# Inverse norms from Ln and Exp on ScalarE, their product with the rotated rows on GpSimd, and other PSUM banks for two results

## What is computed

```
def attn_layer(x, Wqkv, qs, ksc, Wo):
    q, k, v = split into heads of (x @ Wqkv)
    q = l2norm(q) * qs                      # t / max(norm(t), 1e-12), over the 64 of a head
    k = l2norm(k) * ksc
    q = q * cos * scale + rotate_half(q) * sin * scale
    k = k * cos * inv + rotate_half(k) * sin * inv
    out = local_attention(q, k, v)          # softmax over 64 keys, scores times 8
    return out @ Wo
for i in range(6):
    x = attn_layer(shift_tokens(x), Wqkv[i], q_scale[i], k_scale[i], Wo[i]) + x
    x = ffn_layer(shift_tokens(x), ...) + x # layer norm, 128 -> 2 x 341, gelu gate, 341 -> 128
```

## Time and profile before

| | us |
|---|---|
| median of 3 runs | 4887.78 |
| lowest and highest | 4876.82, 4889.48 |
| the profiled execution, its own time | 4899.51 |
| its span, first to last instruction | 4897.4 |
| mean granted TensorE clock over the span | 0.928 of full speed |

### The profile page before, as it was taken

One profiled execution on the slowest core, in us unless ns is written; L12 is line 12 of the kernel. 1 busy time (PEld: TensorE's weight loads), 2 busy tenths in 40 slices (PEclk: granted clock), 3 DMA queues, 4 the chain that ended last, 5 costly groups with the idle time before them and its releaser, 6 DMA issues. The chain is left out here.

```text
span 4897.4 us, 167150 instructions
## 1 busy us (share of the span) xinstructions
PE 4225.8 (86%) x70698; PEld 3385.6 (69%) x70890; DVE 3638.9 (74%) x5894; ACT 2546.2 (52%) x3896; POOL 2850.0 (58%) x2141
## 2 busy tenths in 40 slices
PE   6996899999998999999999999999998658668667
PEld 6885677777777777777777777777775338658447
DVE  4444888888888888888888888888885564564554
ACT  2232456655555555665556555565554326546435
POOL 2223777777777777777777777777773027517025
PEclk9776999999999999999999999999999868868878
DMA  0001222222222322222222222222221021221022
GB/s 24 0 0 38 74 63 62 67 77 70 63 62 61 85 69 62 62 79 72 63 63 66 78 62 68 64 66 66 66 66 36 9 58 43 73 59 44 23 61 74
DMA packets 214198, 281.51 MB, mean 57 GB/s; under 512 B 58878, under 2 KB 103716, under 8 KB 212740
## 3 DMA queue, kind: packets, MB, share of 16 engines
q1 hardware_dynamic: 203972, 251.85, 19.9%
q0 software_dynamic: 9536, 19.55, 1.5%
HBM read 54.88 MB, written 18.28 MB: 15 GB/s over the span
## 5 line engine op out<-in xcount | busy, mean ns | idle before, releaser
L1524 POOL TENSOR_TENSOR local_rot<-local_rot,local_sines 128x512 f32<-128x512 f32 x768 | 955.2, 1277 | 889.4 <-DVE local_sines L1603 889.4
L1532 POOL TENSOR_TENSOR local_inv_norm<-local_norm2c,minus_half 128x16 f32<-128x16 f32 x384 | 1126.6, 2934 | 31.9
L1411 ACT COPY local_v_tile<-local_bank 128x1024 f32<-128x1024 f32 x192 | 195.0, 1016 | 755.1 <-PE local_bank L1186 755.1
L1184 PE MATMUL local_bank<-local_wqkv_hi,local_ys_hi 128*128 128x512 f32 x1152 | 493.2, 428 | 24.8 <-POOL local_ys_lo L1515 10.4
L1260 PE MATMUL local_bank<-ident,local_normed 128*128 128x128 f32 x3072 | 405.9, 275 | 105.7 <-ACT local_probs_t L1421 90.1
L1603 DVE TENSOR_TENSOR local_rot<-local_bank,local_table 128x1024 f32<-128x1024 f32 x384 | 467.1, 1216 | 11.3 <-issue 7.0
L1593 DVE TENSOR_TENSOR local_normed<-local_rot,local_inv_norm 128x1024 f32<-128x1024 f32 x384 | 454.7, 1218 | 19.4 <-issue 11.5
L1603 DVE TENSOR_TENSOR local_sines<-local_bank,local_table 128x1024 f32<-128x1024 f32 x384 | 466.5, 1215 | 0.0
L1608 DVE TENSOR_REDUCE local_norm<-local_squares 128x16 f32<-128x1024 f32 x384 | 463.9, 1209 | 0.0
L1186 PE MATMUL local_bank<-local_wqkv_hi,local_ys_lo 128*128 128x512 f32 x1152 | 455.2, 395 | 0.0
L1185 PE MATMUL local_bank<-local_wqkv_lo,local_ys_hi 128*128 128x512 f32 x1152 | 455.2, 395 | 0.0
(11 more groups left out here) (420 smaller groups left out, 9074.9 us busy)
## 6 DMA issues: line engine op xcount, KB each, us to landing
local_vals<-local_v_tile SPq DMA_DIRECT2D x1152, 130.0 KB
local_vals<-local_v_tile SPq DMA_DIRECT2D x672, 65.0 KB
local_stage<-in_L_ffn_Wqkv SPq DMA_DIRECT2D x6, 1536.0 KB, 7.1
moe_w<-y_rows SPq DMA_DIRECT2D x32, 256.0 KB, 5.1
moe_w<-in_L_ffn_W SPq DMA_DIRECT2D x3, 2048.0 KB, 9.9
x_rows<-moe_rows SPq DMA_DIRECT2D x12, 512.0 KB, 4.0
local_wo<-in_L_ffn_Wo SPq DMA_DIRECT2D x6, 512.0 KB
moe_taken<-x_rows,moe_take POOLq DMA_INDIRECT x149, 2.6
```

The lines of the kernel that those rows point to most:

```text
L1184: nc.tensor.matmul(out, hi, wqkv_hi[:, d0:d1], start=True, stop=False)
L1524: last = nc.gpsimd.tensor_tensor(of_heads(rot, a)[:, :, to], of_heads(rot, a)[:, :, to], of_heads(sines, a)[:, :, of], ALU.add)
L1532: nc.gpsimd.tensor_tensor(inv_norm[:, cols], norm2c[:, cols], g.minus_half[:, cols], ALU.pow).then_inc(q["inv_norms_ready"], 1)
```

## The change

Three things are changed in `local_transformer_phase`.

Banks: the transposed k goes to banks 4 and 5 instead of 0 and 1, weighed values 0 to banks 0 and 1, weighed values 1 to banks 4 and 5. `turn_qk` of k then no longer waits for the copy of the probabilities but for the products of q of tile `k + 2` (banks 4 and 5 are read), and `weigh_values` 0 no longer waits for those products. `att_ready` counts each half of `divide`, so the scores of the next tile wait for the first half only.

Inverse norms: GpSimd guards all 32 norms of a tile in one instruction. ScalarE takes Ln and then Exp with a scale of -0.5 of them, at the end of its pass, after the copies of q and k and ahead of the feed-forward instructions. The powers on GpSimd go. A table set that holds both functions is loaded by name, at the start and after the Gelus of each sequence, in place of the Exp of one column that used to bring its own table.

Product: `normalise` leaves VectorE and is done by GpSimd, a pass earlier, on tile `k + 2`. On VectorE the second sum of squares moves ahead of `divide`, and `add_output` stands between its halves.

```diff
-    QK, QK_TURN = ((4, 5), (6, 7)), ((2, 3), (0, 1))
-    WEIGHED, WO_BANK = ((4, 5), (0, 1)), 2
+    QK, QK_TURN = ((4, 5), (6, 7)), ((2, 3), (4, 5))
+    WEIGHED, WO_BANK = ((0, 1), (4, 5)), 2
...
                 def make_scores(m):
-                    pe.wait_ge(q["att_ready"], tile("att_ready", m - 1))
+                    pe.wait_ge(q["att_ready"], tile("att_ready", m - 1, 1))
...
+                    elif is_tile(m + 1):
+                        pe.wait_ge(q["products_ready"], tile("products_ready", m + 1, 1))
                     else:
-                        pe.wait_ge(q["probs_t_ready"], tile("probs_t_ready", m - 1))
+                        pe.wait_ge(q["att_ready"], tile("att_ready", m - 2))
...
+                def invert_norms(m):
+                    act.wait_ge(q["norms_guarded"], tile("norms_guarded", m))
+                    nc.scalar.activation(log_norm[:], norm2c[:], ACT.Ln).then_inc(q["logs_ready"], 1)
+                    act.wait_ge(q["logs_ready"], tile("logs_ready", m))
+                    act.wait_ge(q["qk_normed"], tile("qk_normed", m - 1))
+                    nc.scalar.activation(inv_norm[:], log_norm[:], ACT.Exp, scale=-0.5).then_inc(q["inv_norms_ready"], 1)
...
-                    nc.scalar.activation(table_pick[:, 2:3], table_pick[:, 0:1], ACT.Exp)
+                    nc.scalar.preload_act_table_set("natural_log_exp_and_others")
...
                         copy_qk(k + 1, 1)
+                    if is_tile(k + 2):
+                        invert_norms(k + 2)
                     if t == 0 and k > 0 and is_seq(n + 1):
...
-                def invert_norms(m, a):
-                    cols = slice(a * HEADS, (a + 1) * HEADS)
-                    pool.wait_ge(q["norms_ready"], tile("norms_ready", m, a + 1))
-                    nc.gpsimd.tensor_scalar(norm2c[:, cols], norm2[:, cols], 1e-24, None, ALU.max).then_inc(q["norms_guarded"], 1)
-                    pool.wait_ge(q["norms_guarded"], tile("norms_guarded", m, a + 1))
-                    nc.gpsimd.tensor_tensor(inv_norm[:, cols], norm2c[:, cols], g.minus_half[:, cols], ALU.pow).then_inc(q["inv_norms_ready"], 1)
+                def guard_norms(m):
+                    pool.wait_ge(q["norms_ready"], tile("norms_ready", m))
+                    nc.gpsimd.tensor_scalar(norm2c[:], norm2[:], 1e-24, None, ALU.max).then_inc(q["norms_guarded"], 1)
+
+                def normalise(m, a):
+                    pool.wait_ge(q["rotated"], tile("rotated", m, a + 1))
+                    pool.wait_ge(q["inv_norms_ready"], tile("inv_norms_ready", m))
+                    pool.wait_ge(q["qk_turned"], tile("qk_turned", m - 1, a + 1))
+                    nc.gpsimd.tensor_tensor(of_heads(normed, a), of_heads(rot, a), inv_norm[:, a * HEADS:(a + 1) * HEADS].unsqueeze(2).to_broadcast([P, HEADS, HD]),
+                                            ALU.mult).then_inc(q["qk_normed"], 1)
...
                     if is_tile(k):
                         centre(k)
-                    if is_tile(k + 1):
-                        normalise(k + 1, 0)
-                        normalise(k + 1, 1)
                     if is_tile(k + 2):
                         products(k + 2, 0)
                         products(k + 2, 1)
                         sum_squares(k + 2, 0)
+                        sum_squares(k + 2, 1)
                     if t == 2 and is_seq(n - 1):
                         ffn_shift(n - 1)
                     if is_tile(k):
-                        divide(k)
-                    if is_tile(k + 2):
-                        sum_squares(k + 2, 1)
+                        divide(k, 0)
                     if is_tile(k - 1):
                         add_output(k - 1)
+                    if is_tile(k):
+                        divide(k, 1)
```

More of the change, by code:

```diff
@@ L1032, in body @@
         norm2c = sb("norm2c", [P, 2 * HEADS])
+        log_norm = sb("log_norm", [P, 2 * HEADS])
         inv_norm = sb("inv_norm", [P, 2 * HEADS])
@@ L1058, in body @@
                     "max_ready": 1, "centred": 1, "qk_normed": 2, "products_ready": 2, "norms_ready": 2,
-                    "sums_inverted": 2, "att_ready": 1, "y_added": 1,
-                    "rotated": 2, "norms_guarded": 2, "inv_norms_ready": 2}
+                    "sums_inverted": 2, "att_ready": 2, "y_added": 1,
+                    "rotated": 2, "norms_guarded": 1, "logs_ready": 1, "inv_norms_ready": 1}
         per_seq = {"ffn_turned": 1, "ffn_back": 1, "gate_done": 3, "a_done": 3, "w2_done": 1,
@@ L1072, in body @@
                    "ffn_turned", "ffn_back", "gate_done", "a_done", "w2_done")
-        ACT_MADE = ("exp_done", "v_copied", "squared", "probs_t_ready", "qkt_copied", "out_copied", "ys_hi_ready", "y_tok_ready", "y_hat_ready", "xn_ready", "gelu_done")
-        DVE_MADE = ("max_ready", "centred", "qk_normed", "products_ready", "norms_ready", "sums_inverted", "att_ready", "y_added",
+        ACT_MADE = ("exp_done", "v_copied", "squared", "probs_t_ready", "qkt_copied", "out_copied", "ys_hi_ready", "y_tok_ready", "y_hat_ready", "xn_ready", "gelu_done",
+                    "logs_ready", "inv_norms_ready")
+        DVE_MADE = ("max_ready", "centred", "products_ready", "norms_ready", "sums_inverted", "att_ready", "y_added",
                     "stats_ready", "aggregated", "var_ready", "shift_ready", "prod_ready", "seq_done")
-        POOL_MADE = ("rotated", "norms_guarded", "inv_norms_ready", "ys_ready", "rstd_ready")
+        POOL_MADE = ("rotated", "norms_guarded", "qk_normed", "ys_ready", "rstd_ready")
         def credit(eng, made):
@@ L1277, in weigh_values @@
                         pe.wait_ge(q["probs_t_ready"], tile("probs_t_ready", m))
-                        if is_tile(m + 2):
-                            pe.wait_ge(q["products_ready"], tile("products_ready", m + 2, 1))
                     elif is_tile(m + 1):
                         pe.wait_ge(q["qkt_copied"], tile("qkt_copied", m + 1))
+                    else:
+                        pe.wait_ge(q["att_ready"], tile("att_ready", m - 1))
                     for j in range(4):
@@ L1550, in _ @@
                     if is_tile(k + 2):
-                        invert_norms(k + 2, 0)
-                        invert_norms(k + 2, 1)
+                        guard_norms(k + 2)
+                        normalise(k + 2, 0)
+                        normalise(k + 2, 1)
             @block.vector
@@ L1587, in centre @@
                                             ALU.subtract).then_inc(q["centred"], 1)
[L1589 to L1594, removed]
                 def products(m, a):
@@ L1608, in sum_squares, with divide @@
                     nc.vector.tensor_reduce(norm2[:, cols], of_heads(squares, a), AX, ALU.add).then_inc(q["norms_ready"], 1)
[L1610 to L1623, removed]
+                def divide(m, i):
+                    weighed = bank[:, WEIGHED[i][0]:WEIGHED[i][1] + 1, 0:4 * (HD + 1)].rearrange("p a (c d) -> p a c d", d=HD + 1)
+                    dve.wait_ge(q["pv_done"], tile("pv_done", m, i + 1))
+                    nc.vector.reciprocal(inv_sum[:, i].unsqueeze(3), weighed[:, :, :, HD:HD + 1]).then_inc(q["sums_inverted"], 1)
+                    dve.wait_ge(q["sums_inverted"], tile("sums_inverted", m, i + 1))
+                    if i == 0:
+                        dve.wait_ge(q["out_turned"], tile("out_turned", m - 1))
+                    nc.vector.tensor_tensor(att[:, i * 512:(i + 1) * 512].rearrange("p (c a d) -> p a c d", a=2, d=HD), weighed[:, :, :, 0:HD],
+                                            inv_sum[:, i].unsqueeze(3).to_broadcast([P, 2, 4, HD]), ALU.mult).then_inc(q["att_ready"], 1)
                 def add_output(m):
```

## The result

The changed kernel takes 4941.45 us (4936.29 to 4949.70, 4 runs), the kernel before on the same chip 4888.63 (4876.82 to 4897.02, 4 runs): ratio 1.0111, 95% interval 1.0086 to 1.0137. That is 53 us slower, where 67 were forecast, inside the range.

The account below looks back on a forecast made before the run. The stage was taken to last as long as TensorE's list and waits. Tiles summed to -0.31 + 2.29 - 0.31 + 0.14 = +1.81 us, times 48 +87, less 20 of "issue": +67, so 4955, range 4850 to 5010.

Parts of the forecast that it names:

- Tile 2: Pass in which y_hat waits for guard, Ln and Exp, delaying `ffn_back`: 17.95 us instead of 15.66, 2.29 lost.
- Tile 3: Pass with the three Gelus: gains 0.31 us from the new banks, length 16.35; Gelus end at 18.5 instead of 17.3.
- Tile 0: V projection waits 0.4 us for the third Gelu's bank; transposes of k come late, 0.14 lost instead of 0.31 gained.
- The normalisations move this chain no further: Chain to the transposes of k: taking 2 x 1.2 us off VectorE gains nothing, since the first product follows the square.
- Tile 1: Transposes of k wait for the products of q instead of the probabilities' copy: 0.31 us gained, length 16.95 instead of 17.26.
- Issue: Gaps before score matmuls without a semaphore, 40.3 us: the longer wait in tile 2 hides 0 to 40, taken as 20.
- GpSimd's products: Two new 128x1024 products on GpSimd: 2.1 to 2.5 us each, against 1.2 on VectorE, fitting in idle time.
- Rival 3: GpSimd becomes the bound in tile 1 if products exceed 4.4 us each; at 5 us, 58 us more, 5013; chance 0.08.
- Rivals 1 and 2: 1: faster, about 4828, y_hat's delay misses TensorE, chance 0.17; 2: no difference, about 4893, rotation 0.83 us earlier, chance 0.15.
- Rival 4: ScalarE table switches drain behind the load, 2.66 us in all; Gelus of tile 3 1.38 later, 66 us more, 5021; chance 0.02.

Follow-up runs that it names:

- filled: The changed kernel with 20 transposes of the identity, result unused, ahead of TensorE's wait for y_hat: 4913.10 us, ratio 1.0034 to the kernel before.
- norms_only: The changed kernel with the old banks and their waits, keeping the new inverse norms, GpSimd product and VectorE order: 5012.05 us, ratio 1.0237 to the kernel before.
- yhat_first: The changed kernel with y_hat and the scaling of the norm ahead of Ln and Exp on ScalarE in tile 2: 4924.96 us, ratio 1.0069.
- shift_only: The changed kernel with the shift ahead of both sums of squares on VectorE, Ln and Exp left ahead of y_hat: ratio 1.0099 to the kernel before.
- yhat_shift: The changed kernel with y_hat ahead of Ln and Exp in tile 2 and the shift ahead of both sums of squares: ratio 0.9875 to the kernel before.

## Why the prediction was right, and where its terms were off

- **Tile 2, the term that decides** (+2.29): measured +2.09 by means, +1.95 by medians. The mechanism was right step by step. From the end of the guard (2049.55) to y_hat (2049.98) it took 0.43 instead of 0.60, and the whole wait was 123.7 us, not 150.
- **Tile 3** (-0.31): measured +0.14, by medians +0.48. The step that failed is the silent one: every duration on TensorE was taken from rows at full clock, although I lengthened a wait on that very engine from 1.0 to 3 us. The filled run prices the clock at 38 us, over two thirds of the net result; without it tile 3 is 0.57 shorter than before, more than my 0.31.
- **Tile 0** (+0.14): measured -0.34 by medians. The V projection did not wait for the third Gelu. In the filled run tile 3 takes 16.50, near my 16.35; there the Gelus are over 18.00 into the pass (medians) and the V projection starts at 18.44. The three Gelus took 1.81 us one behind the other, where I had added up 2.17 from a pass in which they waited for TensorE.
- **"The normalisations move this chain no further"** was read in tile 1 and holds there. In tile 0 the first product started 6.19 us after the scores before and starts at 6.04 now; the sines are over at 8.39, TensorE is free at 8.46 (both in norms_only, whose rows part the two), and hardly a wait is left in tiles 0 and 3.
- **Tile 1** (-0.31): -0.40 by medians; the transposes of k now wait for the sines of q, 26.1 us in 89 instead of some 40, nearly all of it in tiles 1 and 2.
- **"Issue"** (-20): the difference between means and medians of the four tiles says -0.56 us a sequence, 27 us, and the row of the scores fell by 28.9. The guess of half was low. In tile 3, right behind the wait, these gaps add up to 23.0 us before, 13.9 with waits of 2.0 us (yhat_first), 6.8 to 10.9 with waits of 2.3 to 2.7 (changed kernel, norms_only, shift_only) and 24.6 with none (yhat_shift): there a longer wait hides them. The rest of the fall, from 15.3 to 3.8 in tiles 0 and 1, is not the wait's doing: in norms_only, with a wait of 2.3, they stand at 21.6.
- **GpSimd's products**: 1.90 us (1905 ns on the page), below both bounds. Rival 3 needed 4.4. The price did not matter. Twice VectorE's time, the rule of the Trainium skill (GPSIMD Engine Reference, section 4.1), is high for this form: its 1.22 us on VectorE became 1.6 times that.
- **Rivals 1 and 2**: the y_hat wait did reach TensorE, and the rotation kept its 4.98. Rival 4: the load of the table set took no longer than before.

The direction and the cause were foreseen; that the total came within 14 us of the forecast is luck. Two errors nearly cancelled: the clock (38 us too little loss) against terms that were kinder than the sum, by medians tile 0 by 0.5 us a sequence, tile 2 by 0.3, tile 3 without the clock by 0.3 and the gaps by 0.1.

What stays open: what the gaps in the scores are, and why those in tiles 0 and 1 went only where the new banks and the new norms stand together.

## What to carry to other kernels

When a result is handed to an engine that also serves another consumer, look at its list behind the new wait and not at its load: ScalarE was busy for half of the span, and two small instructions of it, placed behind a wait on GpSimd, cost more than 400 us of relief on VectorE brought. Put the instructions whose inputs are ready ahead of the one that waits. When a wait goes, ask for the second cause on the same instruction and for the next consumer on the engine that you reordered: the shift alone gave nothing, y_hat first alone gave 0.4%, both 2.3%, and the division after them another 0.5%.

## What the runs showed of the hardware

- Around the end of a wait of 2.6 us on a TensorE that had been busy, the granted clock falls to half (the 1.2 GHz level) for a few microseconds: at 38 of 48 such waits in the changed kernel, at 28 of 48 with waits of 2.0 us, and at 1 of 48 in the kernel before, whose waits at this place were 0.9 us on average. Twenty idle transposes in the wait left none at it and paid for themselves.
- An addition of a constant to 128x4 numbers on VectorE took 1.10 us instead of 0.17 when it met a running GpSimd product of 1.9 us. SBUF — State Buffer (Trainium skill, section Who interferes with whom) says that the two engines share a pair of ports that one instruction holds to its end, and that `tensor_scalar` can claim it. The rows agree, with a block until the product's end (1056.98 beside 1056.93). A tiny VectorE instruction ahead of a long chain should not be timed into a GpSimd one.
